# Query bias added where the queries leave PSUM, query weights split as they land, and another order of loads and pieces, in a two-layer cross-attention and FFN kernel

## The chip, the cores and the metric

The kernel runs on one core of a Trainium2 chip. The metric is the device time of one execution in microseconds. A core has TensorE (matmuls, shown as PE, its weight loads as PEld), VectorE (DVE), ScalarE (ACT), GpSimd (POOL) and SyncE (SP), which here issues loads and stores. Each engine works through its own queue in order; engines wait for each other by semaphores.

## The reference

Two batches of 1024 tokens of width 256 (`x`), and a context of 77 rows of width 192 per batch. Four steps, each added to x:

```
x += L0_xattn(layernorm(x), ctx)   16 heads of 16; q = xn @ w_q + b_q, k and v from ctx with bias;
                                   softmax(q k / 4) v; then @ w_o + b_o
x += L0_ffn(layernorm(x))          h = relu(t @ w1[0] + b1[0]); y = t + h @ w2[0] + b2[0];
                                   layernorm(y) * gamma + beta
x += L1_xattn(layernorm(x), ctx)   one head of 256, layernorms with gain and bias
x += L1_ffn(layernorm(x))          per token one of 8 matrices W[t] (256 x 256), chosen by position and the
                                   signs of tile_sigs
```

The change touches the first: `q = xn @ w_q + b_q`.

## The kernel before

Tokens are worked in eight groups g = 0..7 of 256 (two blocks i of 128), four groups per batch; `X[:, g, i, :]` holds a group. Every engine's work is a list of named pieces, written out by hand one after the other at the end of the engine's function (`tensor` L516-546, `vector` L950-982, `scalar` L1120-1143, `gpsimd` L1305-1320, `sync` L1339-1382). What is next on an engine is only this list; a piece waits at its head for what it needs, and everything behind it waits too. The PSUM places are given by hand as the last argument of a TensorE piece (four banks PB0 to PB3 and two halves of the score tensor S4, 0 and 1); `hold` (L241) makes the next user of a place wait until its last content has been read.

One group of the first attention runs so. `stats("A", g)` on VectorE (L590: two bn_stats, two bn_aggr), `rs("A", g)` on POOL (L1192: four small operations, among them a pow, that give the scale and the offset), `apply("A", g)` half on VectorE (L613) and half on ACT (L1009) writes the normalised block, `tA(g)` transposes it on TensorE (L337). Products are done in a split form for accuracy: a value is written as a rounded high part (type fp32r) and the rest, and `three` (L254) does high x high, high x low, low x high. So `hi("A", g)` on ACT (L1024) and `lo("A", g)` on VectorE (L628) split the transposed block into XTH and XTL, and `q(g)` (L349) does twelve matmuls with WqH and WqL. The queries leave PSUM by `qh(g)` on ACT (L1031, one copy of 512 columns per partition) and `ql(g)` on VectorE (L634, one subtraction of 512). `sc(g, i, a)` (L359) makes the scores against the masked keys KBH (`kba`, ACT) and KBL (`kbl`, VectorE, L762); `smax` (L641) the maxima, and for a = 1 a subtraction out of PSUM; `ex` (L1037) the exponentials; `ssum` (L657) the reciprocal sums, `en` on POOL (L1244) the product with them; `tE`, `et`, `pv`, `o`, `wo`, `x1` turn, apply and add the result. `B` and `Y` are the two layernorms of the FFN, with `w1`, `hh`, `hl`, `w2`, `y`, `x2`; `C` is that of the second attention (`cs`, `cm`, `cex`, `cp`, `co`, `x3_`), `D` that of the last step (`pc`, `pr`, `pa`, and `put`, which scatters the rows to the output). The pieces `r_...` on all engines work out which token goes to which matrix, and `f_...` fold the weights of the second attention.

The bias of the queries and that of w1 need no operation of their own before: the rows of a layernorm sum to zero, so the last column of the normalised block is overwritten with 1 (`apply` leaves out column 255, L622), the last row of the weights is the bias, and the true last row is subtracted from every other row. `pivot(n)` (L573) does this on VectorE after the loads: n = 0 for the query weights (two scalar_tensor_tensor of 256, with the last row broadcast, WQR), n = 1 and 2 for the two halves of w1 (one of 1024 each). `w_hi(n)` on ACT (L987) then makes the high part and `w_lo(n)` on POOL (L1178) the low part, in pieces of 256 columns; n = 0 is the query weights, 1 and 2 are w1, 3 and 4 are w2. The raw weights share two slots (RAW); a slot is loaded anew when `w_lo` is done with it.

## Time and profile before

| | |
|---|---|
| median of three runs | 276.86 us (275.7 to 277.3) |
| the profiled execution | 275.17 us, span 273.4 us, mean granted clock 0.975 |
| PE busy | 247.7 us, 91% of the span, 2048 matmuls |
| DVE busy | 221.0 us, 81%, 566 instructions |
| ACT busy | 158.9 us, 58%, 502 instructions |
| POOL busy | 200.7 us, 73%, 371 instructions |
| chain that ended last | PE 67%, DVE 12%, POOL 9%, ACT 4%, issue 4% |

```profile
## 2 busy tenths in 40 slices
PE   1977798899799999999999999999999999899960
DVE  2899999999999999945999996797688489868640
POOL 3359989897688976379976577889975585768773
PEclk9977999999999999999999999999999999999995
DMA  6992220002111005502001111311260000011111
```

Each digit is a slice of 6.8 us, the busy share in tenths; PEclk is TensorE's granted clock. Busy time of PE is modelled from the starts of pipelined matmuls, so it shows gaps, not speed. The span is the time between the first and the last instruction of the profiled execution; the execution's own time lies 1.8 us above it. In the rows below, "idle" is the time in which an engine had no instruction, put down to what ended it.

### The profile page before, as it was taken

What the parts mean: (1) busy time and instruction counts of PE and PEld (TensorE: products, weight loads), DVE (VectorE), ACT (ScalarE), POOL (GpSimd) and SP (SyncE); (2) the same over time, 40 slices, a digit from 0 to 9 for tenths busy, and PEclk for the clock granted to TensorE, in tenths of its full rate; (3) what the DMA queues carried; (4) which work ended last, traced back from release to release, by engine and by line L of the source; (5) the groups of instructions that cost most, each with busy time, mean ns of one, the idle gap of its engine ahead of it and who ended that gap; (6) DMA issues with size and microseconds to landing.
All of it is one profiled execution on the core that took longest, in us unless ns stands there. A gap on an engine that the chain in (4) does not pass through costs nothing.

```text
span 273.4 us, 6201 instructions
## 1 busy us (share of the span) xinstructions
PE 247.7 (91%) x2048; PEld 220.9 (81%) x2048; DVE 221.0 (81%) x566; ACT 158.9 (58%) x502; POOL 200.7 (73%) x371
## 2 busy tenths in 40 slices
PE   1977798899799999999999999999999999899960
...
DVE  2899999999999999945999996797688489868640
...
POOL 3359989897688976379976577889975585768773
PEclk9977999999999999999999999999999999999995
DMA  6992220002111005502001111311260000011111
GB/s 175 310 311 67 77 80 0 0 2 80 38 38 42 0 2 182 188 1 41 0 2 58 42 50 49 77 60 40 80 192 2 0 2 0 0 59 41 59 77 77
DMA packets 10957, 17.80 MB, mean 65 GB/s; under 512 B 1510, under 2 KB 7181, under 8 KB 10925
## 3 DMA queue, kind: packets, MB, share of 16 engines
...
## 4 chain that ended last, share of the span: by engine, by line
PE 67%; DVE 12%; POOL 9%; ACT 4%; issue 4%; DMA 1%; POOLq 0%; SPq 0%; DVEq 0%; ACTq 0%
PE PB L258 29%; PE PB L251 12%; PE PB L458 7%; PE S L381 5%; PE PB L393 5%; PE PB L333 4%; PE S L371 4%; POOL E L1248 2%; POOL out_x L1302 2%; ACT E L1051 2%; DMA WKV<-in_w_k 1%; DVE SX L649 1%; POOL W1L L1187 1%; POOL X L1257 1%; DVE HL L676 1%
## 5 line engine op out<-in xcount | busy, mean ns | idle before, releaser
L1248 POOL TENSOR_TENSOR E<-E,SX 128x308 f32<-128x308 f32 x64 | 43.3, 706 | 8.2 <-DVE SX L666 8.2
L1051 ACT ACTIVATE E<-S,SX 128x77 f32<-128x77 f32 x128 | 39.5, 340 | 8.0 <-DVE SX L649 7.9
L258 PE MATMUL PB<-XTH,W1H 128*128 128x256 f32 x128 | 37.6, 294 | 1.6 <-DVE XTL L631 1.6
L258 PE MATMUL PB<-W2H,HH 128*128 128x256 f32 x128 | 37.7, 295 | 0.0
L258 PE MATMUL PB<-XTL,W1H 128*128 128x256 f32 x128 | 36.2, 283 | 0.0
L258 PE MATMUL PB<-XTH,W1L 128*128 128x256 f32 x128 | 36.1, 282 | 0.0
L258 PE MATMUL PB<-W2H,HL 128*128 128x256 f32 x128 | 35.6, 278 | 0.0
L258 PE MATMUL PB<-W2L,HH 128*128 128x256 f32 x128 | 35.6, 278 | 0.0
L1205 POOL TENSOR_TENSOR SM<-SM,nhalf 128x2 f32<-128x2 f32 x40 | 29.0, 725 | 3.1
L1061 ACT ACTIVATE ET<-S 124x640 f32<-124x640 f32 x32 | 22.0, 708 | 14.5 <-PE S L381 14.5
L1074 ACT ACTIVATE HH<-PB 128x512 fp32r<-128x512 f32 x32 | 19.2, 605 | 18.2 <-PE PB L258 18.0
L1051 ACT ACTIVATION_READ_ACCUMULATOR E<-S,SX 128x1 f32 x128 | 28.3, 221 | 0.0
L258 PEld LDWEIGHTS PB<-XTH,W1H 128*128 128x128 f32 x128 | 24.4, 191 | 2.6 <-DVE XTL L631 1.8
L1021 ACT ACTIVATE XN<-X,SM 128x255 f32<-128x255 f32 (+1 forms) x32 | 19.1, 602 | 12.7 <-POOL SM L1211 11.3
L608 DVE BATCH_NORM_STATS2 SM<-X 128x6 f32<-128x256 f32 x64 | 23.8, 414 | 2.0 <-DMA X<-in_x 1.2
L258 PEld LDWEIGHTS PB<-W2H,HH 128*128 128x128 f32 x128 | 24.1, 188 | 1.2 <-issue 1.2
L649 DVE TENSOR_REDUCE SX<-S 128x8 f32<-128x616 f32 x32 | 24.4, 783 | 0.4 <-PE S L371 0.2
L381 PE MATMUL S<-ident,E 128*124 128x128 f32 x160 | 22.0, 274 | 2.9 <-POOL E L1248 2.6
L258 PEld LDWEIGHTS PB<-XTL,W1H 128*128 128x128 f32 x128 | 24.5, 191 | 0.1
L258 PEld LDWEIGHTS PB<-XTH,W1L 128*128 128x128 f32 x128 | 24.5, 191 | 0.0
L258 PEld LDWEIGHTS PB<-W2L,HH 128*128 128x128 f32 x128 | 24.2, 189 | 0.1
L258 PEld LDWEIGHTS PB<-W2H,HL 128*128 128x128 f32 x128 | 24.1, 188 | 0.0
...
## 6 DMA issues: line engine op xcount, KB each, us to landing
RAW<-in_w SPq DMA_DIRECT2D x4, 512.0 KB, 5.4
WD<-in_WD SPq DMA_DIRECT2D x8, 256.0 KB, 5.0
X<-in_x SPq DMA_DIRECT2D x4, 256.0 KB, 7.9
x<-X SPq DMA_DIRECT2D x4, 256.0 KB, 2.1
E<-in_WD SPq DMA_DIRECT2D x4, 256.0 KB, 3.2
...
X<-in_w1r SPq DMA_DIRECT2D x1, 512.0 KB, 8.6
RT<-in_WD SPq DMA_DIRECT2D x2, 256.0 KB, 3.7
```

What stands on the lines that cost most here:

```text
L251: t = e.matmul(dst, a, b, start=j == 0, stop=j == len(pairs) - 1)
L258: t = e.matmul(dst, a, b, start=first and j == 0, stop=last and j == n - 1)
L381: t = e.transpose(P[0:CW, c * 128:(c + 1) * 128], E[:, i, a, c * CW:(c + 1) * CW], ident[:, :])
L458: t = e.matmul(P[:, v * 256:(v + 1) * 256], XP[:, r % 2, v, c * 128:(c + 1) * 128], weights_of(n)[:, c * 256:(c + 1) * 256], start=c == 0, ...
L608: step(e.bn_stats(smi(K, g, i, 0, 6), src[:, i, :]))
L649: e.tensor_reduce(top, sv, AX, ALU.max, negate=True).then_inc(s["mx"], 1)
L1021: e.activation(dst_of(K, g)[:, 1, 0:n], src_of(K, g)[:, 1, 0:n], ACT.Identity, bias=smi(K, g, 1, 10, 11), scale=smi(K, g, 1, 9, 10)).then_ ...
L1051: t = e.activation(Ei[:, h * NK:(h + 1) * NK], P[:, at:at + NK], ACT.Exp, bias=SX[:, i, 0, k:k + 1], accum_out=SX[:, i, 1, k:k + 1])
L1061: e.activation(ET[:, g % 2, a, :, ts], P[0:CW, 0:640].rearrange("p (c t) -> p c t", c=5), ACT.Copy).then_inc(s["et"], 1)
L1074: e.activation(HH[:, 2 * j:2 * j + 2, :], two(bank("w1", g, j)[:, :]), ACT.Relu).then_inc(s["hh"], 1)
L1205: e.tensor_tensor(sm(K, g, 9), sm(K, g, 8), nhalf[:, :], ALU.pow).then_inc(s["rs" + K], 1)
L1248: t = e.tensor_tensor(Eh, Eh, SX[:, i, 2, 8 * a + h:8 * a + h + 4].unsqueeze(2).to_broadcast([128, 4, NK]), ALU.mult)
```

## The change

- `b_q` is now two more columns of `cols`. `qh` adds it as a bias per partition (two activations of 256 columns instead of one copy of 512), and `ql` adds it in a scalar_tensor_tensor per half.
- The query weights are used as they land: no last row, no `pivot(0)`; `w_hi(0)` waits for the load alone, and stands second in ACT's list. Their low part is one subtraction of 512 on VectorE, `wq_lo()`, in place of POOL's `w_lo(0)`. `nkeep` is now made in `pivot(1)`.
- `apply("A", g)` writes all 256 columns, and XN's slot 0 needs no ones.
- Loads: the broadcast row `wqr` goes; the value bias is loaded by itself, for 77 partitions; x's second and third group, and the w1 rows, move forward, `w_o` back; `w1b` waits for `wql`.
- All lists are written anew. No piece but the named ones is added or removed.

```diff
-        cols = sb("cols", [128, 12])
-        COLS = dict(b_k=0, bk1=2, bq1=4, bv1=6, g1=8, be1=10)
+        cols = sb("cols", [128, 14])
+        COLS = dict(b_k=0, bk1=2, bq1=4, bv1=6, g1=8, be1=10, b_q=12)
...
                 w.wait_ge(s["bi" + K], g + 1)
-                if K == "A":
-                    w.wait_ge(s["one"], 1)
-                elif K == "B":
+                if K == "B":
...
-                w.wait_ge(s["wlo"], 1)
+                w.wait_ge(s["wql"], 1)
                 w.wait_ge(s["loA"], g + 1)
                 P = hold(("q", g), ("B", p), ("ql", g + 1))
...
-            keys(3); tA(0, 2); vmat(3); q(0, 2); vrep(0, 3); sc(0, 0, 0, 0); sc(0, 0, 1, 1); r_scores(2); tA(1, 1)
-            sc(0, 1, 0, 1); sc(0, 1, 1, 0); tA(2, 0); q(1, 3); tE(0, 0, 0, 0); vrep(1, 1); tE(0, 0, 1, 1)
...
-            w2(7, 1, 1); pr(0, 1, 1); pr(0, 2, 0); tC(6, 2); pr(0, 3, 3); tD(4, 2); cs(6, 1); pr(0, 4, 0); tC(7, 3)
-            tD(5, 1); cs(7, 2); cp(6, 3); pr(0, 5, 0); cp(7, 1); co(6); co(7); pr(0, 6, 0); pr(0, 7, 2); pr(1, 0, 1)
...
+            keys(1); tA(0, 3); vmat(1); q(0, 2); vrep(0, 0); tA(1, 1); sc(0, 0, 0, 0); sc(0, 0, 1, 1); r_scores(2)
+            sc(0, 1, 0, 1); sc(0, 1, 1, 0); q(1, 3); tA(2, 0); tE(0, 0, 0, 1); tE(0, 0, 1, 0); vrep(1, 1)
...
+            w2(7, 0, 1); w2(7, 1, 0); w2(7, 1, 1); pr(0, 1, 1); pr(0, 2, 2); tD(4, 1); tC(6, 0); pr(0, 3, 3); cs(6, 1)
+            pr(0, 4, 2); tC(7, 0); tD(5, 1); cp(6, 3); cs(7, 0); co(6); pr(0, 5, 0); cp(7, 1); co(7); pr(0, 6, 2)
...
                 w.wait_ge(s["m_id"], 1)
-                if n == 0:
+                if n == 1:
                     step(e.tensor_scalar(nkeep[:, :], ident[:, 127:128].to_broadcast([128, 2]), 1.0, None, ALU.subtract))
                     settle()
-                w.wait_ge(s[("wq", "w1a", "w1b")[n]], 16)
-                w.wait_ge(s[("wqr", "w1r", "w1r")[n]], 16)
-                W, R, by = ((RAW[:, 0, 0:512], WQR, None), (RAW[:, 1, 0:1024], W1R, -1.0), (RAW[:, 0, 0:1024], W1R, keep))[n]
-                if n == 0:
-                    step(e.scalar_tensor_tensor(out=W[:, 0:256], in0=R, scalar=-1.0, in1=W[:, 0:256], op0=ALU.mult, op1=ALU.add))
-                    W, by = W[:, 256:512], keep
-                e.scalar_tensor_tensor(out=W, in0=R, scalar=by, in1=W, op0=ALU.mult, op1=ALU.add).then_inc(s["wfix"], 1)
+                w.wait_ge(s[("w1a", "w1b")[n - 1]], 16)
+                w.wait_ge(s["w1r"], 16)
+                W, by = ((RAW[:, 1, 0:1024], -1.0), (RAW[:, 0, 0:1024], keep))[n - 1]
+                e.scalar_tensor_tensor(out=W, in0=W1R, scalar=by, in1=W, op0=ALU.mult, op1=ALU.add).then_inc(s["wfix"], 1)
+
+            def wq_lo():
+                w.wait_ge(s["whi"], 1)
+                e.tensor_tensor(flat2(WqL[:, :, :]), raw(0), flat2(f(WqH[:, :, :])), ALU.subtract).then_inc(s["wql"], 1)
...
                     w.wait_ge(s["cs"], g) if g else w.wait_ge(s["p_f"], 2)
                 elif K == "D" and g:
                     w.wait_ge(s["tD"], g)
-                n = LAST if K in "AB" else 256
+                n = LAST if K == "B" else 256
                 e.tensor_scalar(dst[:, 0, 0:n], src[:, 0, 0:n], smi(K, g, 0, 6, 7), smi(K, g, 0, 9, 10),
...
                     w.wait_ge(s["sc"], 4 * g - 4)
-                e.tensor_tensor(XTL[:, 1 + g % 2, :, :], two(bank("q", g)[:, :]), f(XTH[:, 1 + g % 2, :, :]),
-                                ALU.subtract).then_inc(s["ql"], 1)
+                for m in range(2):
+                    t = e.scalar_tensor_tensor(out=XTL[:, 1 + g % 2, m, :], in0=two(bank("q", g)[:, :])[:, m, :],
+                                               scalar=col("b_q", m), in1=f(XTH[:, 1 + g % 2, m, :]),
+                                               op0=ALU.add, op1=ALU.subtract)
+                    t.then_inc(s["ql"], 1) if m else step(t)
 
...
                 w.wait_ge(s["p_v"], 1)
-                w.wait_ge(s["bc"], 16)
+                w.wait_ge(s["bv"], 16)
...
-            setup(); mask(); stats("A", 0); apply("A", 0); pivot(0); kf(); lo("A", 0); kbl(0); r_sign(); vs()
-            stats("A", 1); ql(0); vb(0); smax(0, 0, 0); smax(0, 0, 1); stats("A", 2); apply("A", 1); pivot(1)
-            pivot(2); apply("A", 2); ssum(0, 0, 0); lo("A", 1); smax(0, 1, 0); smax(0, 1, 1); ssum(0, 0, 1); r_ranks()
...
-            stats("D", 5); y(7); stats("Y", 7); x2(7); pa(0, 1); stats("C", 7); pa(0, 2); pa(0, 3); apply("D", 5)
-            apply("C", 7); cm(6); pa(0, 4); cm(7); pa(0, 5); x3_(6); stats("D", 6); x3_(7); stats("D", 7)
...
+            setup(); mask(); stats("A", 0); apply("A", 0); wq_lo(); kf(); lo("A", 0); r_sign(); stats("A", 1); vs()
+            kbl(0); apply("A", 1); ql(0); stats("A", 2); pivot(1); smax(0, 0, 0); pivot(2); smax(0, 0, 1); vb(0)
+            ssum(0, 0, 0); lo("A", 1); r_ranks(); apply("A", 2); smax(0, 1, 0); ssum(0, 0, 1); f_stats()
...
+            apply("D", 4); y(7); stats("Y", 7); pa(0, 1); x2(7); pa(0, 2); stats("C", 7); pa(0, 3); cm(6)
+            apply("C", 7); apply("D", 5); pa(0, 4); cm(7); x3_(6); pa(0, 5); stats("D", 6); x3_(7); stats("D", 7)
...
 
-                if n < 3:
-                    w.wait_ge(s["wfix"], n + 1)
+                if n == 0:
+                    w.wait_ge(s["wq"], 16)
+                elif n < 3:
+                    w.wait_ge(s["wfix"], n)
                 else:
...
-                e.activation(XTH[:, 1 + g % 2, :, :], two(bank("q", g)[:, :]), ACT.Copy).then_inc(s["qh"], 1)
+                w.wait_ge(s["cols"], 16)
+                for m in range(2):
+                    t = e.activation(XTH[:, 1 + g % 2, m, :], two(bank("q", g)[:, :])[:, m, :], ACT.Identity, bias=col("b_q", m))
+                t.then_inc(s["qh"], 1)
 
...
-            rep(); apply("A", 0); hi("A", 0); w_hi(0); kba(0); qh(0); kba(1); ex(0, 0, 0); ex(0, 0, 1); apply("A", 1)
-            w_hi(1); hi("A", 1); apply("A", 2); w_hi(2); ex(0, 1, 0); hi("A", 2); ex(0, 1, 1); qh(1); et(0, 0, 0)
...
+            rep(); w_hi(0); apply("A", 0); hi("A", 0); kba(0); qh(0); apply("A", 1); hi("A", 1); apply("A", 2)
+            ex(0, 0, 0); w_hi(1); w_hi(2); ex(0, 0, 1); ex(0, 1, 0); qh(1); ex(0, 1, 1); et(0, 0, 0); et(0, 0, 1)
...
                 w.wait_ge(s["whi"], n + 1)
-                hi_, to = ((flat2(WqH[:, :, :]), flat2(WqL[:, :, :])), (W1H[:, 0, :], W1L[:, 0, :]),
-                           (W1H[:, 1, :], W1L[:, 1, :]), (flat2(W2H[:, 0:4, :]), flat2(W2L[:, 0:4, :])),
-                           (flat2(W2H[:, 4:8, :]), flat2(W2L[:, 4:8, :])))[n]
-                for o in range(0, 1024 if n else 512, 256):
+                hi_, to = ((W1H[:, 0, :], W1L[:, 0, :]), (W1H[:, 1, :], W1L[:, 1, :]),
+                           (flat2(W2H[:, 0:4, :]), flat2(W2L[:, 0:4, :])), (flat2(W2H[:, 4:8, :]), flat2(W2L[:, 4:8, :])))[n - 1]
+                for o in range(0, 1024, 256):
                     if o:
                         w.wait_ge(s["low"], low_made[0])
                     low_made[0] += 1
                     t = e.tensor_tensor(to[:, o:o + 256], raw(n, w=1024)[:, o:o + 256], f(hi_)[:, o:o + 256], ALU.subtract)
-                    t.then_inc(s["low" if o + 256 < (1024 if n else 512) else "wlo"], 1)
+                    t.then_inc(s["low" if o < 768 else "wlo"], 1)
...
-            setup(); rs("A", 0); w_lo(0); r_iota(); bo(0); rs("A", 1); rs("A", 2); bo(1); w_lo(1); en(0, 0, 0)
-            en(0, 0, 1); en(0, 1, 0); w_lo(2); en(0, 1, 1); f_rs(); f_gb(); en(1, 0, 0); en(1, 0, 1); en(1, 1, 0)
...
+            setup(); rs("A", 0); rs("A", 1); rs("A", 2); bo(0); r_iota(); bo(1); en(0, 0, 0); w_lo(1); en(0, 0, 1)
+            en(0, 1, 0); w_lo(2); f_rs(); en(0, 1, 1); en(1, 0, 0); rs("A", 3); f_gb(); en(1, 0, 1); en(1, 1, 0)
...
             load("wk", WKV[:, :, 0:256], chunks("w_k", 96))
             load("wq", two(raw(R_WQ)), chunks("w_q", 128))
-            load("wqr", WQR, A["w_qr"].to_broadcast([128, 256]))
             load("wv", WKV[:, :, 256:512], chunks("w_v", 96))
-            load("sg", sg[:, 0, :], A["sigT"])
-            load("pe", peT, A["peT"])
-            load("bc", bc[:, :, :], A["rows"].rearrange("(a r) n -> a r n", a=1).to_broadcast([128, 6, 256]))
+            load("bv", bc[0:NK, BV, :], A["rows"][BV:BV + 1, :].to_broadcast([NK, 256]))
             load("ldx1", X[:, 1, :, :], x_v[1])
-            load("ldwo", Wo[:, :, :], chunks("w_o", 128))
+            load("sgpe", sg[:, 0, :], A["sigT"])
+            load("sgpe", peT, A["peT"])
+            load("bc", bc[:, 0:BV, :], A["rows"][0:BV, :].rearrange("(a r) n -> a r n", a=1).to_broadcast([128, 5, 256]))
+            load("ldx2", X[:, 2, :, :], x_v[2])
             load("w1r", W1R, A["w1r"].to_broadcast([128, 1024]))
             load("w1a", raw(R_W1, w=1024), A["w1"][0:128, :])
-            load("ldx2", X[:, 2, :, :], x_v[2])
-            w.wait_ge(s["wlo"], 1)
+            w.wait_ge(s["wql"], 1)
             load("w1b", raw(R_W1 + 1, w=1024), A["w1"][128:256, :])
+            load("ldwo", Wo[:, :, :], chunks("w_o", 128))
...
```

## Rows read from the trace of the kernel before

**Rows 1.** The windows of four stretches (length, busy us and instructions per engine, clock, DMA).
```profile
6.00:28.00 22.00, 17.66 (x102) 14.81 (x102) 20.14 (x50) 15.63 (x53) 13.11 (x25) 0.84 0.75 225
28.00:74.00 46.00, 41.40 (x401) 35.23 (x402) 43.70 (x111) 28.80 (x96) 39.23 (x62) 1.00 0.14 41
74.00:236.00 162.00, 161.87 (x1410) 148.81 (x1411) 134.87 (x341) 98.56 (x313) 121.45 (x235) 1.00 0.16 49
```

**Rows 2.** The waits of PE (engine, line, releaser: us in total, times, longest).
```profile
PE S L381 <- POOL E L1248: 2.6, 2, 2.3
PE PB L258 <- DVE XTL L631: 1.6, 1, 1.6
PE PB L258 <- POOL WqL L1187: 0.3, 1, 0.3
```

**Rows 3.** The timeline about 72 to 74 us (start, us, engine, what; idle before).
```profile
71.95 0.28 PE L258 MATMUL PB<-W2H,HL 128*128 128x256 f32 x1
73.83 0.39 PE L258 MATMUL PB<-XTH,W1H 128*128 128x256 f32 x1 [1.59 <-DVE XTL L631]
73.09 0.68 DVE L631 TENSOR_TENSOR XTL<-PB,XTH 128x512 fp32r<-128x512 f32 x1
```

**Rows 4.** The timeline of 6 to 15 us.
```profile
6.04 0.17 DVE L576 TENSOR_SCALAR nkeep<-ident 128x2 f32<-128x2 f32 x1
8.01 0.91 PEld L333 LDWEIGHTS PB<-ident,XN 128*128 128x128 f32 x4
9.86 0.62 ACT L994 ACTIVATE WqH<-RAW 128x512 fp32r<-128x512 f32 x1
10.55 1.65 POOL L1187 TENSOR_TENSOR WqL<-RAW,WqH 128x256 fp32r<-128x256 f32 x2 [4.37 <-ACT WqH L994]
10.63 1.91 DVE L765 TENSOR_TENSOR KBL<-XTE,mask 128x308 fp32r<-128x308 f32 x2
13.99 0.60 ACT L1035 ACTIVATE XTH<-PB 128x512 fp32r<-128x512 f32 x1 [2.25 <-PE PB L258]
14.65 0.66 DVE L638 TENSOR_TENSOR XTL<-PB,XTH 128x512 fp32r<-128x512 f32 x1
```

**Rows 5.** DMA issues at 2.8, 7.2 and 12.2 us (KB, us to landing).
```profile
RAW<-in_w_q SPq DMA_DIRECT2D x1, 256.0 KB, 4.0
RAW<-in_w SPq DMA_DIRECT2D x1, 512.0 KB, 9.3
RAW<-in_w SPq DMA_DIRECT2D x1, 512.0 KB, 7.4
```

**Rows 6.** One line's instructions, L765 (ns shortest, median, longest).
```profile
L765 DVE TENSOR_TENSOR KBL<-XTE,mask x4: 583/992/1008, 10.6 to 53.6; 128x308 fp32r<-128x308 f32 x4
```

**Rows 7.** The timeline of 236 to 248 us, two pairs.
```profile
246.60 0.88 DVE L721 SCALAR_TENSOR_TENSOR X<-PB,PS,X 128x256 f32<-128x256 f32 x2
239.00 1.09 ACT L1021 ACTIVATE XN<-X,SM 128x256 f32<-128x256 f32 x2 [0.98 <-POOL SM L1211]
```

**Rows 8.** The timeline of 16 to 33 us.
```profile
16.11 1.51 DVE L649 TENSOR_REDUCE SX<-S 128x8 f32<-128x616 f32 x2
19.31 0.38 DVE L625 TENSOR_SCALAR XN<-X,SM 128x255 f32<-128x255 f32 x1
28.33 0.77 PE L381 MATMUL S<-ident,E 128*124 128x128 f32 x5 [2.32 <-POOL E L1248]
32.39 1.66 DVE L649 TENSOR_REDUCE SX<-S 128x8 f32<-128x616 f32 x2
```

**Rows 9.** The timeline of VectorE, 36 to 37 us.
```profile
36.05 0.67 DVE L915 TENSOR_SCALAR CKN<-CKN,SM 77x192 f32<-77x192 f32 x2 [0.21 <-POOL SM L1217]
37.05 0.80 DVE L649 TENSOR_REDUCE SX<-S 128x8 f32<-128x616 f32 x1 [0.23 <-PE S L371]
```

**Rows 10.** The timeline of TensorE at 238 us.
```profile
238.57 1.97 PE L458 MATMUL PB<-E,XP 128*128 128x256 f32 x8 [0.93 <-ACT XP L1112]
```

**Rows 11.** The timeline of VectorE at 237 us.
```profile
237.37 1.10 DVE L742 SCALAR_TENSOR_TENSOR X<-PB,MK,X 128x256 f32 x2
```

More of the change, by code:

```diff
@@ L22 @@
 SIGNALS = (
-    "ldx0 ldx1 ldx2 ldx3 ctxT cols wqr w1r wk wv wq sg pe bc ldwo w1a w1b w2a w2b ck gb fWk fWv fWqT fWq fWo " + "".join(f"wd{n} " for n in range(15)) +
+    "ldx0 ldx1 ldx2 ldx3 ctxT cols w1r wk wv wq sgpe bv bc ldwo w1a w1b w2a w2b ck gb fWk fWv fWqT fWq fWo " + "".join(f"wd{n} " for n in range(15)) +
     "gx4 gx5 gx6 gx7 kept sx0 sx1 sx2 sx3 bs out "
     "p_k p_v p_rsc p_rrk p_rpm p_f tA q sc tE pv wo tB w1 w2 tC cs cp co tD pr "
-    "d wfix ranks sub kf kbl vs vb rsg roh rpos route route2 ei varA varB varY varC varD mx "
+    "d wfix wql ranks sub kf kbl vs vb rsg roh rpos route route2 ei varA varB varY varC varD mx "
     "apA apB  apC apD loA ql rc x1 loB hl y x2 ca cm x3 pa d_f "
@@ L954, in vector @@
-            stats("A", 3); f_norm(); ssum(1, 0, 0); smax(1, 1, 0); ql(2); ssum(1, 0, 1); smax(1, 1, 1); x1(0)
-            ssum(1, 1, 0); stats("B", 0); r_position(); smax(2, 0, 0); ssum(1, 1, 1); apply("A", 3); apply("B", 0)
-            f_kv(0); f_kv(1); ssum(2, 0, 0); smax(2, 0, 1); lo("B", 0); kbl(1); smax(2, 1, 0); smax(2, 1, 1); hl(0, 0)
-            ssum(2, 0, 1); hl(0, 1); x1(1); stats("B", 1); r_index(); vb(1); hl(0, 2); apply("B", 1); f_m(); hl(0, 3)
-            lo("A", 3); r_pairs(); lo("B", 1); stats("A", 4); ql(3); y(0); ssum(2, 1, 0); ssum(2, 1, 1); smax(3, 0, 0)
@@ L964, in vector @@
-            ssum(4, 0, 0); hl(2, 2); smax(4, 1, 0); smax(4, 1, 1); ql(5); cm(0); ssum(4, 0, 1); apply("C", 1)
-            hl(2, 3); lo("B", 3); smax(5, 0, 0); apply("A", 6); ssum(4, 1, 0); ssum(4, 1, 1); starts(); y(2)
-            stats("Y", 2); smax(5, 0, 1); hl(3, 0); ssum(5, 0, 0); x2(2); hl(3, 1); smax(5, 1, 0); smax(5, 1, 1)
-            hl(3, 2); hl(3, 3); stats("C", 2); x1(4); stats("B", 4); ssum(5, 0, 1); cm(1); lo("A", 6); ssum(5, 1, 0)
-            ssum(5, 1, 1); apply("C", 2); y(3); stats("Y", 3); x3_(0); x2(3); ql(6); stats("C", 3); cm(2)
@@ new lines, in vector @@
+            ssum(0, 0, 0); lo("A", 1); r_ranks(); apply("A", 2); smax(0, 1, 0); ssum(0, 0, 1); f_stats()
+            smax(0, 1, 1); ssum(0, 1, 0); r_expert(); ql(1); ssum(0, 1, 1); lo("A", 2); smax(1, 0, 0); smax(1, 0, 1)
+            stats("A", 3); f_norm(); ssum(1, 0, 0); ssum(1, 0, 1); smax(1, 1, 0); ql(2); smax(1, 1, 1); x1(0)
+            ssum(1, 1, 0); stats("B", 0); r_position(); smax(2, 0, 0); ssum(1, 1, 1); kbl(1); apply("B", 0); f_kv(0)
+            f_kv(1); smax(2, 0, 1); lo("B", 0); ssum(2, 0, 0); smax(2, 1, 0); smax(2, 1, 1); ssum(2, 0, 1); hl(0, 0)
@@ new lines, in vector @@
+            hl(0, 1); x1(1); apply("A", 3); stats("B", 1); r_index(); hl(0, 2); f_m(); vb(1); hl(0, 3); apply("B", 1)
+            lo("A", 3); r_pairs(); lo("B", 1); ql(3); y(0); ssum(2, 1, 0); ssum(2, 1, 1); hl(1, 0); smax(3, 0, 0)
+            f_q(); smax(3, 0, 1); stats("Y", 0); stats("A", 4); hl(1, 1); hl(1, 2); hl(1, 3); x2(0); ssum(3, 0, 0)
+            stats("C", 0); ssum(3, 0, 1); f_c(); apply("A", 4); smax(3, 1, 0); smax(3, 1, 1); stats("A", 5)
+            stats("A", 6); ssum(3, 1, 0); y(1); apply("A", 5); lo("A", 4); ssum(3, 1, 1); x1(2); stats("Y", 1)
@@ new lines, in vector @@
+            stats("B", 2); ql(4); lo("A", 5); f_o(); stats("A", 7); apply("B", 2); x2(1); smax(4, 0, 0); lo("B", 2)
+            stats("C", 1); apply("C", 0); x1(3); smax(4, 0, 1); hl(2, 0); stats("B", 3); hl(2, 1); hl(2, 2)
+            apply("B", 3); smax(4, 1, 0); ssum(4, 0, 0); smax(4, 1, 1); ql(5); ssum(4, 0, 1); ssum(4, 1, 0); hl(2, 3)
+            cm(0); apply("C", 1); smax(5, 0, 0); lo("B", 3); ssum(4, 1, 1); starts(); hl(3, 0); y(2); apply("A", 6)
+            ssum(5, 0, 0); stats("Y", 2); smax(5, 0, 1); x2(2); hl(3, 1); hl(3, 2); hl(3, 3); stats("C", 2); x1(4)
```

177 lines of the change are left out of this document (85 added, 92 removed).

## The prediction, made before the changed kernel was run

> **What bounds the kernel now.** I read the windows first. From 74 to 236 us TensorE is busy for 161.87 of 162.00 us at full clock; from 6 to 28 us for 17.66 of 22.00, from 28 to 74 us for 41.40 of 46.00 [rows 1]. So TensorE bounds the long middle, and a gain has to come before 74 us or in the tail. VectorE is the other way round: 20.14 of 22.00 and 43.70 of 46.00 us early, 134.87 of 162.00 later [rows 1]. Then the waits of TensorE: 2.6 us for the normalising on POOL, 1.6 for an XTL on VectorE, and only 0.3 for the low part of the query weights, which this change moves [rows 2]. Last the hand-over at the end of the front: TensorE starts its last matmul of a row at 71.95 us, VectorE's XTL (the lo("B", 1) of the code) starts at 73.09, and TensorE's next matmul, w1(1, 0), at 73.83 after 1.59 us of idle time [rows 3]. From there TensorE is full to 236 us. So the length of the front is the time at which VectorE reaches lo("B", 1).
>
> Comparing the two VectorE lists, the same pieces stand ahead of lo("B", 1) before and after, but for pivot(0), gone, and wq_lo(), new. Another order inside that stretch cannot shorten it unless VectorE stops idling. So I sum what is added to VectorE's stretch, and taken from it, between kbl(0) at 10.63 us and lo("B", 1).
>
> **The change part by part.**
>
> *Query weights.* pivot(0) goes and one subtraction of 512 elements comes, at most the 0.68 us of such an XTL [rows 3]. It stands before kf(), which needs the key matmuls and starts at about 8.5 us. w_q, issued at 2.78, lands 4.0 us later [rows 5], its copy to WqH takes 0.62 [rows 4], so wq_lo runs from about 7.5 to 8.2 us in VectorE's idle time. Cost 0; without that cover 0.7. The nkeep step goes behind, in front of pivot(1), into the full stretch: 0.17 us and its wait, +0.2 [rows 4].
>
> *ACT's apply("A", 0)* now stands behind w_hi(0), so it starts when that ends, at 7.45, and takes 0.6. The first transposes began at 8.01 (their weight load) and now begin at about 8.1 [rows 4]: lo("A", 0) and kbl(0) +0.1.
>
> *POOL's w_lo(0)*, 1.65 us, goes [rows 4]. q(0) waited 0.3 us for it [rows 2], so it can gain no more than that; and q(0) is not the bound, since the scores wait for ql(0) and kbl(0) on VectorE. But kbl(0), two products in 1.91 us, ran beside w_lo(0): 0.99 us each, where the same form was as short as 0.58 [rows 4, 6]. Bounds are 1.91 (as now) and 1.2 us; POOL still has an rs() piece beside it, so I take 1.3, a gain of 0.6. The Trainium skill, page GPSIMD Engine Reference, says in its specifications that POOL shares its SBUF interfaces with VectorE and contends with VectorE instructions that have two SBUF inputs; 0.99 against 0.58 us agrees. By it nothing is gained while POOL works beside kbl(0), and the sum would be 0.6 higher.
>
> *ql*, eight times: one subtraction of 512 elements, 0.66 us [rows 4], becomes two scalar_tensor_tensor of 256 from PSUM with a per-partition operand. The nearest row is such a pair, 0.88 us [rows 7]: +0.22 each. Bounds: 0 (as now) and +0.44 (the pair with a wait between its halves, 1.10 us [rows 11]). Three of them (groups 0 to 2) stand ahead of lo("B", 1): +0.66.
>
> *qh*, eight times: one ACT copy of 0.60 us [rows 4] becomes two of 256 with a bias operand. Two of 256 with both bias and scale operands take 1.09 [rows 7]; bounds 0 and +0.5 a pair, I take 0.9. Seven are hidden: TensorE has other pieces between q(g) and the scores. The first is not. q(0) ended where qh(0) began, 13.99 us [rows 4], now at about 13.65; qh(0) then ends at 14.6. VectorE began ql(0) at 14.65; with +0.1, kbl's -0.6 and apply("A", 1) moved ahead of it (0.3 [rows 8]) it comes at 14.45 and waits 0.15. The Trainium skill, page ScalarE: Activation LUTs, What ACT_TABLE_LOAD costs, gives 93 ns for each per-partition operand and 93 ns of overlap back to back; by it a pair is 0.89 us, and the sum is the same.
>
> *Up to 33 us.* smax(1, 0, 0) started at 32.39 us [rows 8], in a stretch with no idle time. Now: +0.1 start, -0.6 kbl(0), +0.22 nkeep, +0.44 for ql(0) and ql(1), +0.15 wait = 32.7, if VectorE never starves. It comes to pivot(1) at 16.6 us and to pivot(2) at 18.6, and both need loads: w1a took 9.3 us from its issue at 7.18, now with 128 KB less before it; w1b took 7.4 us from 12.2 and can go at 8.3 [rows 5]. smax(0, 0, 0) starts near 17.8 instead of 16.11 [rows 8], and the first exponentials as much later. en(0, 0, 0) now precedes w_lo(1) on POOL, but the half of the score bank that tE(0, 0, 0) needs is let go by ex(0, 1, 0), at about 28.0: it starts at 28.1 us, where it started at 28.33 after 2.32 of idle time [rows 8]. So that wait does not go; its releaser changes.
>
> *33 to 74 us.* VectorE idled 0.21 and 0.23 us here [rows 9]; a later VectorE absorbs these, -0.44. ql(2): +0.22. At lo("B", 1): 0.3 + 0.22 - 0.44 = +0.1.
>
> *Middle.* Number and shapes of TensorE's matmuls stay: 0. ql, qh, and the other order there lie beside a full TensorE. *Tail.* TensorE idles 0.93 us before 238.57; the profile names ACT, but VectorE's pair of 237.37 (pa(0, 2), whose bank pr(0, 4) takes) ends 0.1 us earlier [rows 10, 11], and it stood behind stats("C", 7). Now pa(0, 2) comes first, but the statistics then come 1.1 us later, and tC(7), cs(7) and their exponentials hang on them: 0 net, bounds -0.9 and +0.9.
>
> Sum: 273.4 + 0.1 = 273.5 us of span. The profiled execution took 275.17, so 275.3; the median of the three runs is 276.86, 0.6% above it. On the scale of the median: 277.0.
>
> **The rivals.**
>
> *Faster (0.35).* The front loses real idle time. For it: TensorE idles 8.9 us between 6 and 74 us, w_lo(0) no longer competes with VectorE, and POOL's work beside the pivots is spread anew. If lo("B", 1) comes early enough to close the 1.6 us wait, and the tail wins its 0.9, the time is 2.5 less: 274.4. Against: VectorE is 95% busy from 28 to 74 us, and the pieces ahead of lo("B", 1) are the same.
>
> *Slower (0.25).* The pivots ahead of the first score maxima: smax(0, 0, 0) queues behind pivot(1) and smax(0, 0, 1) behind pivot(2). The exponentials start 1.7 us later or more, w_hi(1) and w_hi(2) queue with them on ACT, and ssum, en and tE follow. It decides from the point where w1a lands after 16.6 or w1b after 18.6 us, or where ex(0, 1, 0) ends after 29: then VectorE starves ahead of pivot(2) or ssum. Price: the shift of 1.7 stays, and 0.2 for the waits about it: 278.9. For it: 7.4 us for w1b, if set by the amount in flight, left it no earlier. Against: fewer bytes stand ahead of both.
>
> *The query part does nothing* (inside the likeliest): the 0.3 us removed and the instructions added both vanish in the order, and the time is 276.9.
>
> **How the numbers follow.** A measurement here tells about 0.5% (1.4 us) from no change. Likeliest, no change: 0.40, alone 275.6 to 278.2. Faster than that: 0.35; slower: 0.25. The bounds of ql (0 to +1.3 for three), kbl (-0.7 to 0) and the tail (0.9 either way) are 1.5 to 2 us round 277.0; with most of both rivals the range is 273.9 to 279.2.
>
> **What would show it.** Right: lo("B", 1) starts within 0.7 us of 73.1; VectorE is busy 43 to 45 us of 28 to 74; a ql pair takes 0.85 to 0.9 us, a qh pair 0.9; tE(0, 0, 0) near 28.1, its wait put down to ACT's exponentials; TensorE full from there to about 236. Wrong: w1(1, 0) starting without a wait before 73 us (the faster rival); VectorE idle over 1 us between 15 and 30 us (the slower); or new waits of TensorE between 74 and 236 us, which I put at none.

## The result and the profile after: 280.8 us, 1.35% slower

The changed kernel took 280.77 us (median of four executions, 278.9 to 284.1) against 276.78 us; the ratio is 1.0135, 95% interval 1.008 to 1.019. The ratios here and below leave out executions more than 1.5% above a kernel's shortest. The prediction was 277.0 us, in a range of 273.9 to 279.2. The profiled execution took 278.88 us, span 277.1, beside 275.17 and 273.4: +3.7 us, which the next views place.

The page's slices of the changed kernel (tenths busy; PEclk is TensorE's granted clock):

```profile
PE   1978798899899999989899899999999999999960
DVE  2888998988999999873999997798979577968540
PEclk9985999999999999999999999999999999999995
```

The windows that answer to [rows 1] (busy us of each engine, then granted clock, DMA share, GB/s):

```profile
6.00:28.00 22.00, 19.06 (x102) 16.10 (x102) 18.32 (x48) 12.07 (x41) 13.38 (x24) 0.78 0.74 214
28.00:74.00 46.00, 41.53 (x401) 35.09 (x400) 42.76 (x114) 32.33 (x109) 38.45 (x62) 1.00 0.13 41
74.00:236.00 162.00, 158.89 (x1387) 145.18 (x1388) 138.27 (x339) 99.03 (x316) 120.22 (x232) 1.00 0.16 49
```

Read the third line first. TensorE, full before with 161.87 of 162.00 us [rows 1], now has 3.1 us of gaps there. VectorE has 1.8 us less busy time in the first window, a part of it work that is gone: pivot(0), and 1.06 us of kbl(0). And with the same 102 matmuls TensorE was busy 1.4 us longer before 28 us: its clock was at half (1.2 GHz) from 18 to 28 us, before the change from 17 to 24.

The waits of TensorE from 74 us on answer to [rows 2], where only the first line has a counterpart:

```profile
PE PB L257 <- DVE XTL L629: 1.0, 1, 1.0
PE PB L330 <- DVE X L722: 0.8, 1, 0.8
PE PB L330 <- DVE XN L623: 0.8, 1, 0.8
PE PB L250 <- DVE HL L677: 0.8, 1, 0.8
PE PB L250 <- ACT PTT L1096: 0.5, 1, 0.5
PE PB L330 <- ACT XN L1024: 0.3, 1, 0.3
```

The three of 0.8 us stand at 121, 138 and 157 us: tC(1) waits for VectorE's apply("C", 1), cs(1) for the bank of hl(3, 2), tB(4), behind tA(7), for the bank that x3_(1) reads. VectorE had just gone through its starts(), the loading of 15 values into registers, which the page doesn't count as busy (the kernel before has it too, 6.3 us):

```profile
129.11 0.69 DVE L677 SCALAR_TENSOR_TENSOR HL<-PB,HH 128x512 fp32r<-128x512 f32 x1 [5.83 <-issue]
```

Whether that sets the waits, e8 and e17 below try.

The front, the timeline that answers to [rows 4, 8] (start, us, engine, what; idle before):

```profile
12.91 0.85 DVE L766 TENSOR_TENSOR KBL<-XTE,mask 128x308 fp32r<-128x308 f32 x2
13.72 0.84 ACT L1040 ACTIVATE XTH<-PB,cols 128x256 fp32r<-128x256 f32 x2 [2.42 <-PE PB L257]
14.95 0.87 DVE L637 SCALAR_TENSOR_TENSOR XTL<-PB,cols,XTH 128x256 fp32r<-128x256 f32 x2
17.12 1.54 POOL L1210 TENSOR_TENSOR SM<-SM,nhalf 128x2 f32<-128x2 f32 x1
18.03 0.79 DVE L650 TENSOR_REDUCE SX<-S 128x8 f32<-128x616 f32 x1
20.13 0.60 ACT L1024 ACTIVATE XN<-X,SM 128x256 f32<-128x256 f32 x1 [3.00 <-POOL SM L1216]
20.63 0.31 ACT L1057 ACTIVATE E<-S,SX 128x77 f32<-128x77 f32 x1
29.20 0.74 PE L378 MATMUL S<-ident,E 128*124 128x128 f32 x5 [1.12 <-ACT E L1057]
```

The instructions cost what was forecast: the pair of qh 0.84 us, that of ql 0.87, kbl 0.85. What did not keep its time is the chain behind the maximum at 18.03: the first exponential is at 20.63 us, since ACT's apply("A", 2) stands ahead of it and waits 3.0 us for POOL. At 54 us the front is 1.5 us late: w1(0, 0) starts at 55.52 us, before the change at 54.01.

The hand-over that answers to [rows 3]:

```profile
73.92 0.68 DVE L629 TENSOR_TENSOR XTL<-PB,XTH 128x512 fp32r<-128x512 f32 x1
74.66 0.39 PE L257 MATMUL PB<-XTH,W1H 128*128 128x256 f32 x1 [1.03 <-DVE XTL L629]
```

And the last group of matmuls, first of the kernel before, then of the changed one:

```profile
263.02 1.03 PE L458 MATMUL PB<-OWN,XP 128*128 128x256 f32 x4
```

```profile
266.74 1.03 PE L455 MATMUL PB<-OWN,XP 128*128 128x256 f32 x4
```

This splits the loss. w1(1, 0) starts 0.83 us later (74.66 for 73.83), since the wait ahead of it shrank from 1.59 to 1.03 us. From there to the last group it is 192.08 us for 189.19 before, with the same pieces: +2.89. I call this the length behind w1(1, 0); it is the measure of most experiments below.

### The profile page after: what moved, and what is told of

The parts are those of the page before. It is cut to its first block, busy times and chain, and to the rows that moved or that the text cites. A ratio compares the mean times of both kernels' runs of the same rounds, so it can differ in the third digit from the quotient of the medians.

```text
span 277.1 us, 6218 instructions
## 1 busy us (share of the span) xinstructions
PE 250.5 (90%) x2048; PEld 222.4 (80%) x2048; DVE 224.2 (81%) x573; ACT 161.4 (58%) x510; POOL 200.2 (72%) x369
## 4 chain that ended last, share of the span: by engine, by line
PE 51%; DVE 24%; POOL 7%; issue 7%; ACT 6%; DVEq 2%; DMA 1%; POOLq 1%; SPq 0%; ACTq 0%
PE PB L257 22%; PE PB L250 10%; PE PB L455 5%; PE PB L390 3%; PE S L378 3%; PE PB L330 3%; PE S L368 3%; DVE SM L606 3%; ACT E L1057 3%; POOL SM L1210 2%; POOL out_x L1307 2%; DVE SX L650 2%; DVEq L229 2%; DVE SX L664 2%; DVE HL L677 1%
## 5 line engine op out<-in xcount | busy, mean ns | idle before, releaser
L677 DVE SCALAR_TENSOR_TENSOR HL<-PB,HH 128x512 fp32r<-128x512 f32 x32 | 21.0, 677 | 9.2 <-issue 6.1
L1024 ACT ACTIVATE XN<-X,SM 128x256 f32<-128x256 f32 (+1 forms) x32 | 18.9, 599 | 16.3 <-POOL SM L1216 11.6
```

Source lines behind the costliest of these rows:

```text
L677: e.scalar_tensor_tensor(out=HL[:, hs, :], in0=two(bank("w1", g, j)[:, :]), scalar=0.0, in1=f(HH[:, hs, :]), op0=ALU.max, op1=ALU.subtract ...
L1024: e.activation(dst_of(K, g)[:, 1, 0:n], src_of(K, g)[:, 1, 0:n], ACT.Identity, bias=smi(K, g, 1, 10, 11), scale=smi(K, g, 1, 9, 10)).then_ ...
```

## The experiments

All ratios are to the kernel before, run on the same chip in between.

**1. The query part alone, the order alone, and the two halves of the order.** After cutting both kernels' lists at w1(1, 0) and lo("B", 1), the same pieces stand ahead of the cut on TensorE and VectorE, so halves can be joined.

e1: the changed kernel with the lists and loads of before (`w_hi(0)` stays second on ACT):
```diff
-            setup(); mask(); stats("A", 0); apply("A", 0); wq_lo(); kf(); lo("A", 0); r_sign(); ...
+            setup(); mask(); stats("A", 0); apply("A", 0); wq_lo(); kf(); lo("A", 0); kbl(0); ...
```


> The query bias at the exit from PSUM, the raw query weights and wq_lo on VectorE, but every list and the loads as before the change (without the row that is no longer loaded). If the instructions of the query part cost (the pairs ql take 0.87 us where one took 0.66, eight times, 1.7 us more on VectorE), it lands at 278 to 280 us. If the order of the pieces is what costs, this kernel stays with the kernel before, 275.5 to 277.5 us; TensorE waits under 0.5 us between 74 and 236 us.

Measured: 277.28 us, ratio 1.0027 (0.9996 to 1.0059); length behind w1(1, 0) 189.74. The interval holds 1: no cost of the query part is told from none here.

e2: the kernel before with the new lists and loads; `pivot(0)` in the place of `wq_lo()`, `w_lo(0)` third on POOL, `w_hi(0)` back behind `hi("A", 0)` on ACT.


> The reverse: the kernel before with its way of computing the queries (pivot(0), w_lo(0) on POOL, bias in the last row), and all lists and loads in the changed kernel's order. If the order is what costs: 279 to 281.5 us, with about 3 us of waits of TensorE between 74 and 236 us, on the VectorE pieces apply(C, 1), hl and x3_. If the query part costs: within 1 us of the kernel before.

Measured: 281.17 us, ratio 1.0187 (1.0139 to 1.0235); length 191.64. So the order is what costs, and the query part is near nothing. The profile shows something new, too: a second stretch of half clock (busy, granted clock as above):

```profile
32.00:38.00 6.00, 6.00 (x38) 4.59 (x41) 4.49 (x9) 4.18 (x13) 5.34 (x8) 0.50 0.20 63
```

e3 and e4: new lists up to the cut and old ones behind it, and the reverse.


> The changed kernel until TensorE's w1(1, 0) (about 74 us), and from there on the lists of the kernel before. If the loss arises in the middle's order: 275.5 to 277.5 us and no wait over 0.3 us of TensorE between 76 and 236 us. If it is laid down in the front (TensorE's clock low until 28.2 us instead of 24.2, 1.4 us more of busy time with the same 102 matmuls before 28 us): 279 to 281 us.

> The lists and loads of the kernel before until w1(1, 0), with the new query part, and from there on the changed kernel's lists. If the loss arises in the middle's order: 279 to 281 us with about 2.4 us of waits of TensorE on tC(1), cs(1) and the transposes behind x3_, between 118 and 160 us. If it is laid down in the front: 275.5 to 277.5 us.

Measured: 281.58 us, 1.0157 (1.0111 to 1.0203), and 285.09 us, 1.0321 (1.0278 to 1.0365). By their times both expectations fail: either half is slow beside the other's. Part of that is the joint. The bank of w1(1, 0) is still held for ql(3) in e3, a wait of 3.5 us, and for y(0) in e4, 3.9 us, and half clock follows in both; e3 had half clock from 18.6 to 39.1 us besides.

One cut later the joint and the clock are out of the way. Ahead of w1(2, 0) the same pieces stand on TensorE in all lists, and from there to the last group the granted clock is full in all four kernels. Its first matmul, in the kernel before, the changed one, e3 and e4:

```profile
104.89 0.47 PE L258 MATMUL PB<-XTH,W1H 128*128 128x256 f32 x1
105.72 0.43 PE L257 MATMUL PB<-XTH,W1H 128*128 128x256 f32 x1
112.38 0.47 PE L257 MATMUL PB<-XTH,W1H 128*128 128x256 f32 x1
111.08 0.44 PE L257 MATMUL PB<-XTH,W1H 128*128 128x256 f32 x1
```

The last groups start at 263.02, 266.74, 270.82 and 271.95 us, so the length behind w1(2, 0) is 158.13 us before, 161.02 in the changed kernel, 158.44 in e3 and 160.87 in e4. Behind it e3 has no wait of TensorE over 0.4 us ahead of the tail, and e4 has the three of the changed kernel, at 0.8, 0.8 and 0.7 us.

So what both expectations said of the middle holds, though the times hide it: the loss there goes with the lists behind w1(1, 0), whichever lists stand ahead of them.

**2. Local repairs of the changed kernel.** e5: on ACT, `ex(0, 0, 0)` ahead of `apply("A", 2)`. e6: also `ex(0, 0, 1)`, and on VectorE `smax(0, 0, 0); smax(0, 0, 1)` ahead of `stats("A", 2); pivot(1); pivot(2)`.


> The changed kernel with one move on ACT: ex(0, 0, 0) ahead of apply(A, 2), which waited 3.0 us for POOL's small operations until 20.13 us. If this wait is what makes the front late and keeps TensorE's clock low until 28.2 us (and, in the order-only kernel, again from 31.8 to 38 us): the exponentials start near 18.8 us, the clock is back by 25 us, tE(0,0,0) stands near 28.5, no second low stretch, and the time falls to 278 to 279.5 us. If the middle's order alone costs: unchanged, 280 to 281.5 us.

> As the kernel before it, and also ex(0, 0, 1) ahead of apply(A, 2), and on VectorE both maxima of the first block, smax(0,0,0) and smax(0,0,1), ahead of stats(A, 2) and the two pivots (my slower rival of the prediction undone). If the pivots ahead of the maxima cost: the first exponentials at about 16.8 us as before the change, and 277.5 to 279 us, with 2 to 3 us of waits left in the middle. If they don't: within 0.5 us of the kernel with ACT's move alone. The low part of w1 gets later by some 1.5 us, which w1(0, 0) does not feel.

Measured: 283.69 us, 1.0296 (1.0185 to 1.0406), and 286.51 us, 1.0297 (1.0191 to 1.0403). Neither gain came. The exponentials did start earlier, at 18.65 and 19.43 us. In e5 lo("A", 1) came earlier too, at 22.23 us for 23.33, but TensorE waited 2.7 us for ACT ahead of tE(0, 0, 0), and its clock was at half from 28.0 to 38.3 us. In e6 lo("A", 1) came later (TensorE waits 3.3 us for it at 26 us), and half clock lasted from 23.1 to 36.8 us. The waits of the middle stand as before in both, so neither ACT's move nor the pivots ahead of the maxima, my slower rival, make them. Whether the pivots cost in the front, e6 can't say, since it brought losses of its own there.

e7: three swaps in TensorE's list, one at each 0.8 us wait.
```diff
-            tC(1, 1); tE(4, 0, 1, 1); ... cs(1, 2); sc(5, 1, 1, 1); ... tB(4, 3); tC(3, 0);
+            tE(4, 0, 1, 1); tC(1, 1); ... sc(5, 1, 1, 1); cs(1, 2); ... tC(3, 0); tB(4, 3);
```


> The changed kernel with three swaps in TensorE's list, one at each new wait of the middle: tC(1) behind tE(4,0,1), sc(5,1,1) ahead of cs(1), tC(3) ahead of tB(4). If these waits are TensorE's order alone, they go, 2.3 us, and the time falls to 278.3 to 279 us. If they only show that VectorE is late there, other waits take their place, and the time stays at 280 to 281.5 us.

Measured: 283.84 us, 1.0251 (1.0166 to 1.0337), above both ranges. The three waits shrank, but its profile has a wait of 2.06 us at w1(1, 0) and half clock behind it; e13 below is the same edit without that.

e8: `starts()` of VectorE from behind `ssum(4, 1, 1)` to a place ahead of `x3_(3)`.


> The changed kernel with VectorE's starts() (15 register loads, 5.8 us without an instruction from 123.3 us) moved behind hl(4, 3), ahead of x3_(3), where VectorE waits 2.2 us for TensorE anyway. If VectorE's lag behind starts() makes the waits on hl (137.6 us, 0.8) and x3_ (156.9, 0.8): both go, and about 3.5 us of VectorE's lag turn up near 175 us, where TensorE has room or not: 278.5 to 280 us. If they come from the order alone, no change: 280 to 281.5 us.

Measured: 288.53 us, 1.0435 (1.0359 to 1.051). The expectation fails. The wait on hl went and that on x3_(1) fell to 0.45 us, but TensorE waited 3.0 us for an x3_ at 182 us, and half clock followed there too. Up to 123 us its instructions are those of the changed kernel, and still it goes otherwise at w1(1, 0). The windows 76 to 86 us of four profiled executions: the changed kernel, e8, the changed kernel again (e9 below), and e12 below:

```profile
76.00:86.00 10.00, 10.00 (x89) 9.68 (x90) 9.49 (x24) 7.79 (x27) 7.01 (x13) 1.00 0.10 28
```

```profile
76.00:86.00 10.00, 10.00 (x52) 9.68 (x52) 7.58 (x20) 5.02 (x22) 4.86 (x8) 0.50 0.09 26
```

```profile
76.00:86.00 10.00, 8.07 (x45) 7.74 (x46) 7.70 (x17) 3.90 (x19) 6.55 (x9) 0.66 0.09 26
```

```profile
76.00:86.00 10.00, 10.00 (x90) 9.68 (x90) 9.50 (x24) 7.79 (x27) 6.95 (x12) 1.00 0.10 28
```

In the second TensorE is "busy" for all 10 us and does 52 matmuls, where it did 89. Ahead of these windows e8 and e9 waited twice as long at w1(1, 0) as the first profile (1.03 us):

```profile
75.73 0.39 PE L257 MATMUL PB<-XTH,W1H 128*128 128x256 f32 x1 [2.04 <-DVE XTL L630]
```

```profile
77.93 0.39 PE L257 MATMUL PB<-XTH,W1H 128*128 128x256 f32 x1 [2.07 <-DVE XTL L629]
```

**3. The clock.** e9 is the changed kernel unaltered. In e10 and e11 `r_pairs()`, the routing work of 6.5 us that stands ahead of `lo("B", 1)` on VectorE in both kernels, is cut in two:
```diff
-            lo("A", 3); r_pairs(); lo("B", 1);
+            lo("A", 3); r_pairs(); lo("B", 1); r_pairs2();
```
e12 fills TensorE's waits with products that nobody reads:
```diff
+            def fill(n, p):
+                w.wait_ge(s["m_id"], 1)
+                P = hold(("fill",), ("B", p))
+                for _ in range(n):
+                    e.matmul(P[:, 0:128], ident[:, :], ident[:, :], start=True, stop=True)
...
-            keys(1); ... tA(1, 1); ... sc(0, 1, 0, 1); ... tE(0, 0, 0, 1); ... w1(1, 0, 2)
+            fill(12, 1); keys(1); ... fill(4, 1); tA(1, 1); ... fill(4, 3); sc(0, 1, 0, 1); ... fill(4, 1); tE(0, 0, 0, 1); ... fill(4, 2); w1(1, 0, 2)
```


> The changed kernel unaltered, beside the next three on one chip. If the stretches of TensorE's low clock decide its time, its runs spread from 279 to 284 us and their times follow the mean granted clock (0.970 gave 278.9, 0.952 gave 284.1 us); the median is 280 to 284 us. If the order alone costs, its runs stay within 1 us of each other.

> The kernel before, with VectorE's r_pairs() cut in two and lo(B, 1) put between the halves: it comes some 4 us earlier, so TensorE's wait of 1.6 us ahead of w1(1, 0) goes. Nothing else is moved. If this wait only costs itself: 274.5 to 276.5 us. If it also brings the low clock in some executions (mean clock 0.965 instead of 0.975 to 0.981): the runs at 277 to 278 us go as well, and the median is 273.5 to 275.5 us. If VectorE, full there, makes TensorE wait elsewhere: 275.5 to 278 us.

> The same cut of r_pairs() around lo(B, 1) in the changed kernel. In two executions of the same list up to there TensorE waited 1.03 us (no low clock behind it) and 2.04 us (half clock from 76 to 86 us). If such a wait brings the low clock: no low stretch between 74 and 90 us in the profile, and the median 2 to 4 us under that of the unaltered kernel. If the low clock there has another cause: within 1 us of it.

> The changed kernel with matmuls of the identity by itself, read by nobody, where TensorE waits: 12 ahead of keys, 4 each ahead of tA(1), sc(0,1,0), tE(0,0,0) and w1(1,0), each 0.2 us at full clock, so that the waits (6.2, 1.1, 1.2, 1.1 and 1.0 us) are mostly filled. If idle TensorE is what brings its low clock: the mean granted clock rises above the unaltered kernel's by 0.01 or more, and the time falls by 2 to 4 us. If the low clock comes from elsewhere: no gain, up to 1.5 us of loss by matmuls that don't fit in their gap.

Measured: e9 ratio 1.0109 (1.0059 to 1.0159); seven executions at 278.5 to 286.6 us, median 281.8 (an eighth, of 493 us, is left out), the two at a mean clock of 0.970 the shortest, the two at 0.942 and 0.946 at 286.6 and 284.8, but one at 0.963 at 285.2 and one at 0.959 at 280.0: the clock goes with the time, loosely. Its profiled execution took 285.16 us. e12: 278.88 us, ratio 1.0108 (1.0072 to 1.0144), all six executions at 278.75 to 279.50, mean clock 0.971 to 0.980. So the fill took 3 us off the median and left the ratio where it was: the longest executions are the clock's, the 1.1% are not. The spread is not gone for good: e13 and e17, with the same fill, have one execution of six each at 282.6 and 282.9 us. e10: 276.06 us, 1.0005 (0.9975 to 1.0035); e11: 281.47 us, 1.0199 (1.0159 to 1.0239), not the 2 to 4 us under e9 that were expected. Cutting r_pairs() removed the wait at w1(1, 0), and the next piece that needs VectorE waited 1.4 us (e10, sc(3, 0, 0) for ql(3)) or 1.6 us (e11). e11's profile has no half clock behind w1(1, 0), but in the front it lasts from 19.6 to 33.2 us.

**4. What is left with TensorE's early waits filled.** e13 is e12 with the three swaps of e7; e14 is the kernel before with a fill (12 ahead of keys, 6 of tA(1), 5 of tE(0, 0, 0), 5 of w1(1, 0)); e15 is e1 with this fill; e16 is e10 with this fill.


> The changed kernel with the fill and the three swaps in TensorE's list (tC(1) behind tE(4,0,1), sc(5,1,1) ahead of cs(1), tC(3) ahead of tB(4)). If the 2.9 us that are left are the three new waits of TensorE (0.8 us each): 276.5 to 277.5 us. If the swaps only move the waits: 278.5 to 279.5 us as with the fill alone.

> The kernel before with such a fill: 12 matmuls of the identity ahead of keys, 6 ahead of tA(1), 5 ahead of tE(0,0,0), 5 ahead of w1(1,0). If its slower runs (277 to 279 us at a mean clock of 0.965 to 0.968) come from the clock: they go, and all runs lie at 274.5 to 276 us. If the fill only helps an order that starves TensorE early: no change, 275.5 to 276.5 us with the same spread.

> The query part with the lists and loads of before, and the same fill. Against the kernel before with the fill it gives the price of the query part without the noise of the clock: 0 to 0.5 us if the pairs of ql and qh are hidden under the full TensorE, 1 to 1.7 us if VectorE's eight longer pairs (0.87 us for 0.66) are not.

> The kernel before with the fill and with lo(B, 1) between the halves of r_pairs(). Alone the cut of r_pairs() gave nothing (276.1 us), as the wait of 1.6 us ahead of w1(1,0) was followed by one of 1.4 us ahead of sc(3,0,0). If both together free TensorE: 273.5 to 275 us. If the later wait takes all: as the kernel before with the fill, within 0.5 us.

Measured: e13 279.95 us, 1.014 (1.0095 to 1.0185). Its waits of TensorE from 74 us on, but for three more of 0.2 us:

```profile
PE PB L250 <- ACT PTT L1103: 0.5, 1, 0.5
PE PB L257 <- DVE X L679: 0.4, 1, 0.4
PE PB L336 <- DVE X L729: 0.4, 1, 0.4
PE PB L336 <- ACT XN L1031: 0.3, 1, 0.3
PE PB L250 <- DVE HL L684: 0.2, 1, 0.2
```

Each wait of 0.8 us became two small ones, together 0.4 to 0.7 us, all but one of them behind VectorE. The length behind w1(1, 0) is 192.34 us all the same, for 191.93 in e12. TensorE's own order at these three places is not the cause.

e14 276.54 us, 1.0016 (0.9985 to 1.0047); e15 277.43 us, 1.0033 (1.0004 to 1.0062); e16 274.55 us, 0.9938 (0.9913 to 0.9964). e14's executions lie at 275.2 to 279.1 us, so the fill did not take the spread of the kernel before away, and its expectation fails. e15 is 0.9 us above e14, between its two ranges. In e16 the two changes that did nothing alone, the fill and the cut of r_pairs(), together beat the kernel before by 0.6%. Its profile does not say where: the span is 273.3 us, before 273.4. Its two longest waits of TensorE from 74 us on:

```profile
PE PB L464 <- ACT XP L1121: 0.9, 1, 0.9
PE PB L251 <- ACT XN L1087: 0.3, 1, 0.3
```

**5. Is it VectorE's load?** e17 is e12, e18 is e16, each with VectorE's half of apply for A 3, A 4, A 5, C 0 and C 1 done by ACT:
```diff
+                if (K, g) in ON_ACT:
+                    e.activation(dst_of(K, g)[:, 0, 0:n], src_of(K, g)[:, 0, 0:n], ACT.Identity, bias=smi(K, g, 0, 10, 11),
+                                 scale=smi(K, g, 0, 9, 10)).then_inc(s["ap" + K], 1)
```


> The changed kernel with the fill, and VectorE's half of apply for A 3, A 4, A 5, C 0 and C 1 (0.63, 0.83, 0.45, 0.48 and 0.40 us, 2.8 in all) done by ACT, right ahead of its own half. If VectorE's lag sets the waits of TensorE between 118 and 160 us: they fall from 2.5 us to under 1 us, and the time from 279.0 to 276.5 to 277.5 us. If not VectorE but something else paces TensorE there (POOL, the order): 278.5 to 279.5 us.

> The kernel before with the fill, with lo(B, 1) between the halves of r_pairs(), and with the same five halves on ACT. TensorE already is full there from 74 to 236 us, so VectorE's lag costs nothing that shows: if TensorE alone bounds it, 274 to 275 us as without the relief; if small gaps behind VectorE (under 0.3 us each) are left, 273 to 274 us.

Measured: e17 279.68 us, 1.0142 (1.009 to 1.0194). Its longest waits from 74 us on:

```profile
PE PB L259 <- DVE XTL L639: 1.9, 1, 1.9
PE PB L338 <- DVE X L732: 0.8, 1, 0.8
PE PB L252 <- ACT PTT L1109: 0.5, 1, 0.5
```

The wait for apply("C", 1) went and that for hl fell to 0.2, yet the length behind w1(1, 0) only fell from 191.93 to 191.35 us, and w1(1, 0) came later (76.27 us). So 2.8 us less on VectorE gave 0.6. It gave more where the waits are: from w1(2, 0) to w1(4, 0) it is 57.03 us, for 58.38 in e12, and 0.7 us of that was lost again behind w1(4, 0). e18: 274.88 us, 0.9965 (0.9934 to 0.9997), no better than e16, which stays the best version.

The length behind w1(1, 0), in us, where no half clock followed it:

| old lists | | new lists | |
|---|---|---|---|
| before | 189.19 | changed | 192.08 |
| e1 | 189.74 | e2 | 191.64 |
| e14 | 189.23 | e12 | 191.93 |
| e15 | 189.59 | e13 | 192.34 |
| e16, e18 | 189.42, 189.63 | e17 | 191.35 |

Where it did follow, in the changed kernel again (e9) and in e7, it is 195.12 and 195.04.

The length from w1(2, 0) on has no half clock in it but in e8, and sorts all the profiles by the lists behind w1(1, 0), in us:

| lists behind w1(1, 0) | kernels | w1(2, 0) to w1(4, 0) | w1(2, 0) to the last group |
|---|---|---|---|
| old | before, e1, e3, e10, e14, e15, e16, e18 | 55.5 to 55.8 | 158.1 to 158.6 |
| new | changed, e2, e4, e5, e6, e7, e9, e11, e12, e13 | 57.4 to 58.6 | 160.6 to 161.5 |
| new, VectorE relieved | e17 | 57.0 | 160.3 |
| new, starts() moved | e8 | 56.9 | 165.6, with a second half clock |

In the kernel before and the changed one the first column is 55.57 and 58.38 us: 2.81 of the 2.89 us are lost between 105 and 164 us.

The start of w1(1, 0) differs more. With the old lists ahead of it and no joint it lies at 72.7 to 74.9 us in seven profiles. With the new ones it lies at 74.5 to 77.9 us in nine (changed, e2, e7, e8, e9, e11, e12, e13, e17), and the profile that the result section reads, 74.66, is near the best of them. e9, the same kernel, was 3.27 us later there and lost 3.04 us more behind it. In e2, e3 and e5 half clock held on or came back until 38 to 39 us, and TensorE did 53 matmuls from 28 to 38 us, where it did 75 in the changed kernel. No kernel with the old lists in front had this, but for 3.4 us in e16. Why it comes in some executions and not in others, no run here shows.

## Why the prediction was wrong, point by point

- *Query weights, start.* Right: wq_lo ran in VectorE's idle time, at 7.72 us. lo("A", 0) at 10.12 was 0.1 us later, as forecast.
- *kbl(0).* It gained 1.06 us, not 0.6: the pair took 0.85 us at 12.91. Beside it POOL had only an addition of two columns, and that one paid: 1.44 us, where such an addition took 0.20 at 16.84. The prediction's case in which nothing is gained while POOL works beside kbl(0) did not come.
- *ql and qh.* Right: 0.87 and 0.84 us (forecast 0.88 and 0.9). The whole query part, with the old lists, costs 0.3% by e1 and 0.3% by e15 (0.9 us above e14 beside it), at the edge of what the runs tell; by the length behind w1(1, 0) it is 0.4 to 0.6 us. I had it at nothing to 0.3 us. The eight longer pairs of VectorE are 1.7 us.
- *Up to 33 us.* Wrong. I had smax(1, 0, 0) at 32.7 us if VectorE never starves; it came at 34.07. VectorE starved: 13.98 busy of the 15 us from 15 to 30, for 14.62 before. The pivots (16.85 and 18.75 us for 16.6 and 18.6) and the maximum of 18.03 (17.8) came as forecast; what I left out is ACT's list, where apply("A", 2) stands ahead of the first exponential, and POOL's chain for it, whose pow took 1.54 us beside pivot(1); before the change group 1's took 0.70 beside vb(0), and group 2's 1.55. I had put tE(0, 0, 0) at 28.1 us; it came at 29.20, its wait put down to ACT's exponentials, as forecast.
- *33 to 74 us.* lo("B", 1) at 73.92 for the forecast 73.2 (73.1 plus 0.1), w1(1, 0) 0.83 us later for 0.1. The front's error is 0.7 us in this profile, and up to 3.3 us more in others with its lists.
- *Middle.* The step that failed: "ql, qh, and the other order there lie beside a full TensorE", 0. It measured +2.9 us behind w1(1, 0), tail included, 2.8 of them between w1(2, 0) and w1(4, 0). The text itself had named the sign, new waits of TensorE between 74 and 236 us. A full TensorE in the kernel before came of its order: the new order was judged by the old one's fullness. I never walked the new lists behind 74 us.
- *Tail.* 0 was right within its bounds: the wait of 0.9 us at 238.57 [rows 10] is gone, and 0.3 and 0.5 us at 244 and 250 us came. It is in the 2.9.
- *Why the new lists leave gaps there.* Shown: it is the lists behind w1(1, 0), with either front (e3, e4); it is not the query part (e1, e15), not TensorE's order at its three waits (e13), not the clock (e12). VectorE's lag is about half of the 2.8 us between w1(2, 0) and w1(4, 0): with five pieces' halves taken off it (e17) or starts() moved away (e8) that stretch lost 1.35 and 1.47 us of its 58.38. Both gave it back later, e17 in part, e8 with far more. The other half stays open. The lists of ACT and POOL are new there too, and 93 of TensorE's 246 pieces have another place in PSUM; no run changes one of these alone.
- *The clock* was no term of the sum at all. It doesn't carry the ratio, but it carries single executions, by 3 us where a stretch follows w1(1, 0), and with them the median: 281.8 us in e9, 278.9 with the fill.
- *The rivals.* The faster one failed at its first condition, an early lo("B", 1). (Its price should read 274.5 us, 2.5 less than 277.0.) The slower one named 278.9 us, what the profiled execution took, and that is luck in the main. Its signs came: VectorE idled 1.02 us between 15 and 30 us, ex(0, 1, 0) ended at 29.0, and smax(1, 0, 0) was 1.7 us late, at 34.07 for 32.39. But 0.83 us of this was left at w1(1, 0), and the 2.9 us behind it, which the rival does not know, made up the rest.
